# Sixteen attention units alone, then eight feed-forward tiles, instead of chunks between the units

## The reference

```
x = x + sequence_block(norm(x))   # causal convolution, running means, GELU MLP
x = x + ffn(norm(x))              # 8 experts, width 512: sum of (silu(h Wg) * (h Wu)) Wd
x = x + attention(norm(x))        # 16 heads of width 8, linear position bias, causal
x = x + ffn(norm(x))              # the same 8 experts, same weights
```

```
scores = q k^T / sqrt(8) + slope_h * (key position - query position), keys after the query hidden
out = softmax(scores) v ; heads side by side, then a 128 x 128 projection
```

## Time and profile before

| | |
|---|---|
| median of three runs | 1768.47 us (1764.17 to 1769.37) |
| the profiled execution | 1763.52 us, of which 1761.8 us from first to last instruction |
| TensorE, matmul | busy 1687.4 us (96%) |
| VectorE | busy 1256.1 us (71%) |
| ScalarE | busy 1038.6 us (59%) |
| GpSimd | busy 477.5 us (27%) |
| mean granted clock of TensorE | 0.990 |

### The profile page before, as it was taken

One profiled execution on the slowest core, in us unless ns is written; L12 is line 12 of the kernel. 1 busy time (PEld: TensorE's weight loads), 2 busy tenths in 40 slices (PEclk: granted clock), 3 DMA queues, 4 the chain that ended last, 5 costly groups with the idle time before them and its releaser, 6 DMA issues.

```text
span 1761.8 us, 27913 instructions
## 1 busy us (share of the span) xinstructions
PE 1687.4 (96%) x10265; PEld 1097.9 (62%) x10265; DVE 1256.1 (71%) x2134; ACT 1038.6 (59%) x1690; POOL 477.5 (27%) x647
## 2 busy tenths in 40 slices
PE   5899999999999999988889999999999999999998
PEld 3567777777777877633345555555555555558877
DVE  7677577666866777778867777777877777646665
ACT  6445755655565555477755666666666666665554
POOL 6522001100210123421124434434433444440000
PEclk8999999999999999989999999999999999999999
DMA  7000011002000132233100000000000000010000
GB/s 215 0 1 1 0 37 25 1 1 64 1 1 1 43 112 60 85 90 92 50 24 14 25 25 26 2 25 25 22 16 25 25 2 1 2 31 1 6 7 6
DMA packets 63427, 52.42 MB, mean 30 GB/s; under 512 B 7984, under 2 KB 58559, under 8 KB 63295
## 3 DMA queue, kind: packets, MB, share of 16 engines
q1 hardware_dynamic: 63120, 50.57, 10.1%
q10 hardware_dynamic: 174, 0.07, 0.0%
HBM read 32.40 MB, written 18.22 MB: 29 GB/s over the span
## 4 chain that ended last, share of the span: by engine, by line
PE 83%; DVE 8%; ACT 4%; issue 2%; SPq 1%; DMA 1%; POOL 0%; DVEq 0%; ACTq 0%; POOLq 0%
PE ps L1278 8%; PE ps L1241 8%; PE ps L1279 6%; PE ps L1280 6%; PE ps L1133 6%; PE ps L1135 6%; PE ps L1134 6%; PE ps L1106 5%; PE ps L1310 4%; PE ps L1075 3%; PE ps L1312 3%; PE ps L1311 3%; PE ps L862 3%; PE ps L1140 3%; PE ps L1142 3%; PE ps L1141 3%
## 5 line engine op out<-in xcount | busy, mean ns | idle before, releaser
L1651 ACT ACTIVATE pr<-ps 128x1024 f32<-128x1024 f32 (+2 forms) x285 | 268.4, 944 | 189.3 <-PE ps L1063 114.3
L2119 DVE TENSOR_TENSOR hid<-sg,ps 128x512 f32<-128x512 f32 x256 | 174.7, 683 | 181.2 <-PE ps L1135 132.0
L822 POOL TENSOR_TENSOR h_lo<-hid,h_hi 128x512 fp32r<-128x512 f32 x176 | 225.6, 1282 | 265.6 <-ACT h_hi L1751 261.1
L1657 ACT ACTIVATE sg<-ps 128x512 f32<-128x512 f32 x256 | 153.5, 600 | 229.8 <-PE ps L1135 227.6
L2109 DVE TENSOR_REDUCE negp<-ps 128x2 f32<-128x1024 f32 (+2 forms) x224 | 254.1, 1145 | 48.4 <-PE ps L1063 32.6
L1133 PE MATMUL ps<-xn_hi,w_hi 128*128 128x512 f32 x512 | 226.8, 443 | 1.8 <-DVE xn_lo L1908 1.8
L1278 PE MATMUL ps<-xn_hi,w_hi 128*128 128x512 f32 x512 | 223.5, 436 | 0.7 <-DVE hid L2246 0.5
L2246 DVE SCALAR_TENSOR_TENSOR hid<-sg,ps 128x512 f32<-128x512 f32 x176 | 121.0, 687 | 126.9 <-ACT sg L1741 126.2
L1279 PE MATMUL ps<-xn_lo,w_hi 128*128 128x512 f32 x512 | 202.2, 395 | 0.0
L1135 PE MATMUL ps<-xn_hi,w_lo 128*128 128x512 f32 x512 | 201.9, 394 | 0.0
L1280 PE MATMUL ps<-xn_hi,w_lo 128*128 128x512 f32 x512 | 201.7, 394 | 0.0
(11 more groups left out here) (244 smaller groups left out, 3085.9 us busy)
## 6 DMA issues: line engine op xcount, KB each, us to landing
qs<-qd SPq DMA_DIRECT2D x60, 96.0 KB
ks<-kd SPq DMA_DIRECT2D x60, 96.0 KB
kd<-qkp SPq DMA_DIRECT2D x14, 256.0 KB, 2.9
qd<-qkp SPq DMA_DIRECT2D x7, 384.0 KB, 2.6
w_raw<-in_Wg SPq DMA_DIRECT2D x4, 512.0 KB, 7.4
w_raw<-in_Wu SPq DMA_DIRECT2D x4, 512.0 KB, 7.5
w_raw<-in_Wd SPq DMA_DIRECT2D x4, 512.0 KB, 9.2
work<-hd SPq DMA_DIRECT2D x8, 256.0 KB, 4.8
```

The lines of the kernel that those rows point to most:

```text
L822: g.tensor_tensor(h_lo[:, q % 2, :], hid[:, q % 4, :], h_hi[:, q % 2, :].bitcast(F32), ALU.subtract).then_inc(FS[1]["hlo_pool"], 1)
L1651: a.activation(pr_of(n, st)[:].rearrange("p (e a) q -> p e a q", e=2)[:, :, hps[0]:hps[-1] + 1, 0:WIDTH[st]], heads(buf, hps, WIDTH[st]), ...
```

## The change

All 16 units run through `unit`, with the ring of three double banks and three probability buffers. No chunk lies between them. The last unit has no next unit: it issues no maxima jobs and no reductions, and it now prepares tile 0. Then `ffn_alone` runs all 256 chunks in the form that `rest_of_ffn` had: Silu, one product, and VectorE's rest. The tanh form and GpSimd's rest are gone. The remains of unit 15 (last values, context, two projections) go ahead of chunk 0 and between chunks 3 to 7.

```diff
-MIX = 5
+LAST_UNIT = UNITS - 1
...
         def pr_of(n, st):
 
-            return (pr0, pr1, pr_third)[st % PR] if n < MIX else (pr0, pr1)[st % 2]
+            return (pr0, pr1, pr_third)[st % PR]
...
-                if n >= MIX:
-                    buf = ps[:, S_BANK:S_BANK + 2, :]
-                    pe.wait_ge(T["exp"], n * NG_S + k)
-                    if n == MIX and k == 0:
-                        pe.wait_ge(T["reduced"], (n + 1) * NG_S)
-                else:
-                    buf = ring(n, SCORE_POS[k])
-                    read_to = issued_to(n, SCORE_POS[k] - BUFFERS)
-                    if read_to[0] > 0:
-                        pe.wait_ge(T["exp"], read_to[0])
-                    pe.wait_ge(T["reduced"], read_to[1])
+                buf = ring(n, SCORE_POS[k])
+                read_to = issued_to(n, SCORE_POS[k] - BUFFERS)
+                if read_to[0] > 0:
+                    pe.wait_ge(T["exp"], read_to[0])
+                pe.wait_ge(T["reduced"], read_to[1])
...
                     if q == 0:
-                        pe.wait_ge(T["ctx"], MIX * 2 - 1)
-                    if 0 < q <= BESIDE:
-                        pe.wait_ge(f["half"], q)
-                    if q == BESIDE + 1:
+                        pe.wait_ge(T["ctx"], UNITS * 2 - 1)
                         pe.wait_ge(T["exp"], UNITS * NG_S)
-                    if q >= BESIDE + 2:
+                    if q >= 2:
                         pe.wait_ge(f["prod"], q - 1)
                     from_input(q, 0, bank(gate_bank(q)), "gate")
...
                     w, dst = slice(c * P, (c + 1) * P), bank(Y_BANK)
                     pe.wait_ge(f["hhi"], q + 1)
-                    if q < BESIDE:
-                        pe.wait_ge(f["hlo_pool"], q + 1)
-                    else:
-                        pe.wait_ge(f["hlo"], q - BESIDE + 1)
+                    pe.wait_ge(f["hlo"], q + 1)
...
-                        if k == 17 and n == MIX - 1:
-                            pe.wait_ge(T["m_out"], n * 2 + 3)
+                        if k == 16 and n == LAST_UNIT:
+                            pe.wait_ge(T["m_out"], n * 2 + 2)
+                            pe.wait_ge(T["ctx"], n * 2)
                             input_T(0, 7)
                         if k == own_T(n):
-                            pe.wait_ge(T["m_out"], n * 2 + 3)
-                            if n == MIX - 1:
+                            if n == LAST_UNIT:
                                 pe.wait_ge(f["xlo"], 1)
+                            else:
+                                pe.wait_ge(T["m_out"], n * 2 + 3)
                             result_T(n, 1)
-                        for job in range(max(JOBS_TO[k], 1 if n == 0 else 0), JOBS_TO[k + 1]):
-                            next_max(n, job)
+                        if n < LAST_UNIT:
+                            for job in range(max(JOBS_TO[k], 1 if n == 0 else 0), JOBS_TO[k + 1]):
+                                next_max(n, job)
                         values(n, k)
 
-                def unit_beside_ffn(n):
...
+                def ffn_alone():
+
+                    for q in range(CHUNKS):
                         c, t = q % CH, q // CH
+                        if q == 0:
+                            values(UNITS, 0)
+                            values(UNITS, 1)
                         for kind in (GATE, UP, DOWN):
                             piece(q, kind)
-                        if q == BESIDE:
-                            values(UNITS, 0)
-                        if q == BESIDE + 3:
+                        if q == 3:
                             pe.wait_ge(T["ctx"], UNITS * 2 - 1)
                             result_T(UNITS - 1, 0, J_BANK)
-                        if q in (BESIDE + 4, BESIDE + 6):
-                            context_T(B - 1, (q - BESIDE - 4) // 2, J_BANK)
-                        if q in (BESIDE + 5, BESIDE + 7):
-                            project_out(B - 1, (q - BESIDE - 5) // 2, J_BANK)
-                        if c == Y_AT[1]:
+                        if q in (4, 6):
+                            context_T(B - 1, (q - 4) // 2, J_BANK)
+                        if q in (5, 7):
+                            project_out(B - 1, (q - 5) // 2, J_BANK)
+                        if c == Y_AT[1] and t:
                             result_of_tile_T(t - 1)
...
-                for n in range(MIX):
+                for n in range(UNITS):
                     unit(n)
-                for n in range(MIX, UNITS):
-                    unit_beside_ffn(n)
-                rest_of_ffn()
+                ffn_alone()
...
-                        if k == 17 and n == MIX - 1:
+                        if k == 16 and n == LAST_UNIT:
                             input_out(0, 7)
...
+                def ffn_alone():
+                    for q in range(CHUNKS):
                         c, t = q % CH, q // CH
+                        if c == Y_AT[0] and t:
+                            result_of_tile_out(t - 1)
                         silu(q)
-                        if c == Y_AT[0]:
-                            result_of_tile_out(t - 1)
-                        first_of_chunk(q - 1)
-                        if q == BESIDE + 1:
+                        if q:
+                            first_of_chunk(q - 1)
+                        if q == 1:
                             result_out(UNITS - 1, 0)
-                        if q in (BESIDE + 4, BESIDE + 6):
-                            context_out(B - 1, (q - BESIDE - 4) // 2, J_BANK)
+                        if q in (4, 6):
+                            context_out(B - 1, (q - 4) // 2, J_BANK)
                         if c == XT_AT and t + 1 < TILES:
...
-                        if (n, k) != (0, 0):
+                        if (n, k) != (0, 0) and n < LAST_UNIT:
                             reduce_job(k, ring(n, JOB_POS[k]), (n + 1) * NG_S)
...
-                        if n == MIX - 1:
+                        if n == LAST_UNIT:
                             if k in (8, 9):
...
+                def ffn_alone():
+                    for q in range(CHUNKS):
                         c, t = q % CH, q // CH
                         product(q)
-                        if q > BESIDE:
+                        if q:
                             rest_of_chunk(q - 1)
-                        if q == BESIDE + 3:
+                        if q == 3:
                             normalise(UNITS - 1, 0, J_BANK)
-                        if q in (BESIDE + 5, BESIDE + 7):
-                            add_projection(B - 1, (q - BESIDE - 5) // 2, J_BANK)
-                        if c == Y_AT[1]:
+                        if q in (5, 7):
+                            add_projection(B - 1, (q - 5) // 2, J_BANK)
+                        if c == Y_AT[1] and t:
                             add_tile(t - 1)
```

More of the change, by code:

```diff
@@ L95, in own_T @@
 def own_T(n):
-    return 18 if n == MIX - 1 else 17
+    return 18 if n == LAST_UNIT else 17
 JOBS_TO = [sum(JOBS_AT[:k]) for k in range(NG_S + 1)]
@@ L101 @@
 BUFFERS = 3
-MIX = 5
+LAST_UNIT = UNITS - 1
 CHUNKS = TILES * CH
 GATE, UP, DOWN = range(3)
[L107 to L122, removed]
+J_BANK, Y_BANK, O_BANK = 2, 4, 6
 def gate_bank(q):
-    return 5 if q < BESIDE or q % 2 == 0 else 0
+    return 5 if q % 2 == 0 else 0
 def up_bank(q):
-    return 7 if q < BESIDE or q % 2 == 0 else 1
+    return 7 if q % 2 == 0 else 1
 Y_AT, STATS_AT, NORM_X_AT, XT_AT = (2, 4), 22, 24, 26
@@ L835, in _ @@
                         third_part(LAST, 1)
-                    if n == MIX - 1 and st == SUB + 1:
+                    if n == LAST_UNIT and st == SUB + 1:
                         norm_of_tile(0)
-                    if st == 2 * SUB - 1:
+                    if st == 2 * SUB - 1 and n < LAST_UNIT:
                         split_max(n * 2 + 2)
-            for n in range(MIX, UNITS):
[L841 to L854, removed]
+            for t in range(1, TILES):
                 norm_of_tile(t)
@@ L1324, in values @@
                     for st in range(len(STEPS)):
-                        if n and values_at(n - 1)[st] == NG_S + k:
+                        if n and VALUES_AT[st] == NG_S + k:
                             weigh(n - 1, st)
                     for st in range(len(STEPS)):
-                        if n < UNITS and values_at(n)[st] == k:
+                        if n < UNITS and VALUES_AT[st] == k:
                             if st == 0:
@@ L1383, in unit @@
                                 project_out(b - 1, (k - 9) // 3)
-                        if k == NEXT_MAXIMA:
+                        if k == NEXT_MAXIMA and n < LAST_UNIT:
                             if n == 0:
@@ L1787, in unit @@
                             maxima_copy(n * 2 + 1)
-                        if k == PLACE:
+                        if k == PLACE and n < LAST_UNIT:
                             place_values((n + 1) // NG, (n + 1) % NG)
@@ L1793, in unit @@
                             result_out(n, 1)
```

(32 more changed lines are left out.)

115 lines of the change are left out of this document (1 added, 114 removed).

## The result

The changed kernel takes 1754.14 us (median of five runs, 1750.19 to 1756.63); the kernel before takes 1766.16 us (median of five). The ratio is 0.993, with a 95% interval of 0.991 to 0.995: 12 us faster, where 4.9 were forecast. The time lies at the low edge of the stated range, 1754 to 1771. The direction held; the gain was over twice the forecast, and most of it came from an order of two instructions that the sum passed over and from spells at a lower clock.

A forecast was written before the change was run, and what follows sets the result against it. TensorE, busy 96% of the span, was taken as the bound beside chunks. Five terms, 290.7 + 18.9 + 31 + 74 + 340.8, gave 755.4 us against 760.3, 4.9 less; prediction 1763.5 us, range 1754 to 1771 (8 in 10).

The forecast's parts named there:

- Term 1: Units 4 to 14 run alone: eleven unit lengths of 26.43 us, 290.7 us in all.
- a sign of being wrong: Any ordinary unit over 27 us, clock below 0.98 in units, VectorE's rest waited for, or a first score awaiting loads.
- Term 2: Three joins of a batch, in units 4, 8 and 12: 6.3 us extra each, 18.9 us in all.
- the spell: TensorE at a lower clock, as in unit 4's join: a join costs about 6.6 us with it, 5.1 without.
- cheap-joins rival: Without statistics a join costs 5.1 us and unit 15 with its start 27: 12.5 us gained, 1756 us; chance 0.20.
- Term 3: From the copy in unit 14 through unit 15 to the first chunk: 31 us, bounds 26 and 37.
- the gaps of the ring: In unit 15, at k = 1, 8, 16 and 18, a score waits for the exponential just before, some 0.5 us each.
- Term 4: First tile, until its result is copied after 34 rounds: 74 us, bounds 72.5 and 77.
- Term 5: Five more tiles, from copy to copy: 68.16 us each, 340.8 us in all, trusted to 0.5 us.
- nothing changes from the sixth tile on: The last 70 us of the kernel were taken to be the same program before and after the edit.
- the stretch: From the copy in unit 3 to the sixth tile's result copy: 760.3 us before, forecast at 755.4.
- The opening of the prediction: A unit beside 16 chunks costs 27.6 to 28.1 us on top of them, against 26.43 alone.

The follow-up runs named there:

- copy_behind: Changed kernel with one edit undone: ScalarE copies a tile's result out behind that round's Silu, as before the change; 1757.07 us, ratio 0.9957.
- mix9: Kernel before with MIX = 9 in place of 5: units 0 to 8 alone, seven units beside chunks; 1766.86 us, ratio 1.0008.
- copy_ahead: Kernel before with only one edit: a tile's result is copied out ahead of Silu where chunks run alone; ratio 0.9992.

## Why the forecast was right in kind and wrong in size

**Term 1, the eleven unit lengths, held.** Forecast 26.43 each, measured 26.43 to 26.54. Units 6 and 10, with the load of values beside them, took 26.54 and 26.53. The queue delivered a unit every 26 us, but with less to spare than the prediction read: in units 13 and 15 the first score waited for its loads, which the prediction had named as a sign of being wrong.

```profile
1129.98 0.39 PE L1066 MATMUL ps<-qs,ks 63*128 63x512 bf16 x2 [0.78 <-DMA qs<-md]
1182.94 0.39 PE L1066 MATMUL ps<-qs,ks 63*128 63x512 bf16 x2 [0.83 <-DMA qs<-md]
```

It cost under 0.1 us each, since the first score waits about as long in the other units, 0.74 us, for an exponential.

**Term 2, the joins, was too dear by 2.4 us** (18.9 forecast; measured 16.2 in the joins and 0.3 more in the ordinary units). The change took the statistics out and with them, nearly always, the spell. I kept most of the spell ("as the holes stay mostly there"); without it the forecast had 5.1, and 5.4 was measured. The cheap-joins rival was right on this point. Its total, 12.5 us, is close to the measured 12 by luck: it had nothing for the copy (5.7) and put 4 us on unit 15, where term 3 was off by 1.6.

**Term 3, unit 15, was too dear by 1.6 us**: 31 forecast, 29.39 measured, and all but 0.4 of it is the spell that I added. The steps of it (ScalarE the leader, the gaps of the ring, the stop for tile 0's input) are in the profile, and the missing gaps were worth 1.3 where I had put 2.

**Term 4, the first tile, held in number, with luck**: 74 forecast, 73.79 measured. The stage ends at the result's copy, which now comes earlier in its round; in the run copy_behind, with the old order that the forecast had in mind, the same stage took 74.98 us, also at a clock of 1.00:

```profile
1204.13:1279.11 74.98, 74.80 (x342) 60.59 (x338) 47.73 (x85) 40.10 (x73) 1.22 (x2) 1.00 0.00 1
```

The term was 1 us short, and the order made up for it.

**Term 5 is the step that failed**: "from copy to copy" 68.16, five times. It was read from the trace of before, as if the loop of that stage stayed the same. The diff changes it: the copy of a tile's result goes ahead of Silu. Before, at the copy that the earlier trace rows show, it stood behind Silu and TensorE waited for it:

```profile
1623.44 0.60 ACT L1745 ACTIVATE sg<-ps 128x512 f32<-128x512 f32 x1 [0.97 <-PE ps L1280]
...
1624.66 0.47 PE L1310 MATMUL ps<-h_hi,w_hi 128*128 128x512 f32 x1 [0.59 <-ACT yS L1736]
```

Measured 67.31 (67.69 for the first of the five), and 336.9 for the five instead of 340.8; over the whole program the edit is worth 5.7 us. The same mistake stands in the sentence that nothing changes from the sixth tile on.

Together 2.4 + 1.6 + 0.2 + 3.9 = 8.1 us, which is 755.4 less 747.3. The other way round, the stretch and what follows it gained 13.4 us: 5.7 from the copy, about 3.0 from two spells which the profiled execution of before had (1.46 in unit 4, and 1.5 in unit 5, on the way into the chunks, 55.47 us at a clock of 0.97 against 53.96 at 1.00 for mix9's unit 9; copy_ahead has the second spell too), 0.75 from the statistics, and the rest, about 4, from the layout itself. The last is what the change is named for. It is a third of the gain, and it is thin: units 6 to 13 with four tiles took 496.3 us beside one another and come to 494.8 in turn (six units of 26.44, two joins of 31.82, four tiles of 68.14), 1.4 us for eight units. The other 2.6 or so lies at the two ends, in units 5, 14 and 15 and the first tile; no run takes it apart.

The opening of the prediction overstated the mixing. It charged a unit beside chunks with 27.6 to 28.1 us; 0.9 of that is the tile's own transposes and waits, which come back alone. The sum had them in its tiles, so no term was wrong by it.

## What to carry to other kernels

When a stage is moved and made longer, price it from the code after, line by line, even where the trace of before shows "the same" stage: an order of two instructions, repeated at seven tile changes, was worth more than the move. A filler between steps and deeper buffering of the steps are two ways to the same end; compare them with all per-tile work on both sides, and expect the difference to be small when the engine is near 96% busy already. In a profile taken once, look for spells of the lower clock before a stage's length is used as a price, and count them apart.

## What the runs showed of the hardware

The same code takes two lengths before the change begins, and they go with the clock granted near the start of the program. Of the thirteen profiles with stages, eight have a granted clock of 0.93 between 50 and 100 us and their copy in unit 3 at 863.66 to 866.16 us; five have 0.83 or 0.86 there and the copy at 869.83 to 870.09. The difference of 5 to 6 us in the spans of the changed kernel (1748.7 and 1754.6) is nearly complete at that point. It belongs to the start of the program, not to the change, and is as large as the gain that was forecast. Both plain joins with a spell fall in the two executions with 0.83; no run shows why.
